# Moving part of a short causal convolution from VectorE to TensorE in a fused delta-rule attention and mixture-of-experts layer

## The chip, the cores and the metric

One core of one Trainium2 chip runs the whole layer in one launch. The metric is the device time of the kernel in microseconds (us). What tells a change of this kernel from no change is about 0.5%.

## The reference, cut to what matters

The layer has two halves. The first is a gated linear attention by the delta rule, the second a router with 32 experts and a shared expert. The change touches only the start of the first half: the projections of the normalised input `x` (2 x 1024 tokens, 512 wide) are convolved along the tokens with four taps that all channels share, and go through SiLU.

```
def _causal_shared_conv(x, w):
    xp = jnp.pad(x, ((0, 0), (K - 1, 0), (0, 0)))
    out = w[0] * xp[:, 0:T, :]
    for j in range(1, K):                      # K = 4 taps
        out = out + w[j] * xp[:, j:j + T, :]
    return out
q = _silu(_causal_shared_conv(x @ Wq, conv_q))
k = _silu(_causal_shared_conv(x @ Wk, conv_k))
v = _silu(_causal_shared_conv(x @ Wv, conv_v))
beta = jax.nn.sigmoid(x @ Wb)
# keys and queries to unit length; per chunk a triangular matrix M of key products is inverted;
# a state S runs over the chunks: u -= w S, o = q S + attn u, S += k^T u; norm, Wo, residual
```

After it come a norm, the router (top groups, top 4 of 32 experts, each expert with room for 80 tokens), the experts and the shared expert.

## The kernel before, in words

**Steps and bodies.** The 1024 tokens are taken in 8 steps of 128 (both batch rows at once). All work is in fp32. A *body* `s` is one turn of the loops on every engine. Body `s` runs the serial core of step `s-1` (four chunks `j` of 32 tokens), prepares step `s` (convolution, SiLU, key products, inverse), projects step `s+1`, and finishes steps `s-2` and `s-3` (output projection, shared expert). Body 0 has no core. Bodies 0 to 7 prepare a step and so hold an inverse; body 8 does not. Then a second block does the routing tables and the 32 experts.

**PE's order is written out by hand.** `FILL` (L64) has 16 strings, four for each chunk of the core. In chunk `j` PE does in this order: state times keys (L497), string `4j`; the solve with the inverse (L512, waits for VectorE's `residual`), string `4j+1`; the state update (L520), string `4j+2`; the output (L526), string `4j+3`. Each letter is a piece of other work: B the beta projection, X the transposes of `x`, P a part of a projection (12 pieces a step, L468; two fill a bank of PSUM), G one quarter of the key and query products (L481), W the output projection (L549), E, F, V, Y the shared expert, H and R for the router, O a small sum. `FILLS` has other strings for single bodies. `Ring` hands six PSUM banks to the pieces in the order in which they stand; a piece waits until the last user of its bank has released it.

**The path of one projection.** PE fills a bank (P). ACT in `take_projection` copies it to `pre` (L703, behind three columns of the step before, the halo) and once more, scaled by the last tap, to `cv` (L704). VectorE adds three taps on `cv` (`conv`, three instructions at L942) and copies the halo (L953). ACT makes the sigmoid in `silu_factor` (Exp, Ln, Exp; L668 to L670). VectorE multiplies: `silu_kq` (L960) for keys and queries, `silu_v` (L965) and then `turn_v` (L968) for values. PE makes the G pieces when both keys and queries are there. VectorE masks them (L980), transposes them for the inverse in `problems` (L985), inverts them with about 30 small instructions and a few large ones (L1017 to L1030), and turns the inverse back (L1044).

**VectorE's order** in a body, as the code has it: `residual(0)` (L1068), conv of keys, conv of queries, `next_state(0)`, `silu_kq` of keys, first tap of values, `silu_kq` of queries, moments of the finished output and `mean_shift` (L1096), `residual(1)`, the other taps of values, masks with `next_state(1)` between them, `problems`, `silu_v`, `turn_v`, `residual(2)`, and the inverse. In body 0 it also does `first_norm(2)` (L916, L929: the layer norm of step 2's input) and scales `wo` (L1205).

**ACT's order** in a body begins with `take_beta`, `take_x`, `take_new(0)`, the sigmoid of keys, the sigmoid of queries, `take_output(0)`, `rstd(1)` (L663), `scale_y`, the first projections, and later the sigmoid of values. Every engine takes its own instructions in this order.

Of the kernel before, what the change touches and what calls it, by code (L numbers as in the profile page):

```python
# [26 lines left out]
P = 128  # L27
# [32 lines left out]

PIECES = dict(X=1, H=1, O=1, G=4, P=12, W=8, E=8, F=8, V=4, Y=4)
BANKS = dict(X=2, H=2, O=2, G=4, P=6, W=2, E=2, F=2, V=1, Y=1)

FILL = ["BXRWW", "WWW", "WWW", "PP", "GPP", "GFF", "GFF", "GFF", "FFPP", "HPP", "PP", "VVVV", "YYYY", "PP", "", "EEEEOEEEE"]  # L64
FILLS = {0: ["BGGGGXPPPPPPPPPPPP"],
         STEPS: ["RWWW", "WWW", "WW", "F", "FF", "F", "F", "FF", "FH", "VV", "V", "VY", "YYY", "EE", "E", "EEOEEE"], STEPS + 1: ["RWWWWWWWWFFFFFFFFHVVVVrYYYYEEEEEEEE"]}


def step_of(body, section):

    if section in "XP":
        return body + 1
    if section in "BG":
        return body
    if section == "O":
        return body - 1
    if section in "WHEr":
        return body - 2
    return body - 3


def pieces_of(body):

    done = dict.fromkeys("BRrXHOGPWEFVY", 0)
# [55 lines left out]
def step_part(nc, ctx, dram, shared):  # L140
# [10 lines left out]
    route_m, pick_of, w_part = shared["route_m"], shared["pick_of"], shared["w_part"]  # L151
    ffn_w, late = shared["ffn_w"], shared["late"]

    wqkv = wring[:, :].rearrange("p (s k n) -> p s k n", s=3, k=KT)
# [104 lines left out]
    v_turned = sem("v_turned")  # L259
    halo_done = sem("halo_done")  # L260
    kq_ready = sem("kq_ready")
# [37 lines left out]
    def quad(n):  # L299
        return slice(DK * n, DK * n + DK)  # L300

    block = ctx.enter_context(nc.Block())
# [130 lines left out]
    def _(pe):  # L433
# [24 lines left out]
        def project(s, n, c):  # L458
# [11 lines left out]
            if c == 1:  # L470
                m.then_inc(ring.full("P", s, n), 1)

        def gram(s, j):

            kq = kqs[s % 2]
            pe.wait_ge(kq_ready, 2 * (s + 1))
            ring.wait_free(pe, "G", s, j)
            bank = ring.bank("G", s, j)
            for i in range(I8):
                for hh in range(HT):  # L480
                    m = te.matmul(bank[quad(hh), i * 64:(i + 1) * 64], kq[quad(hh), i * J + j, 0, :], kq[quad(hh), i * J + j, :, :].rearrange("p a c -> p (a c)"),  # L481
                                  start=True, stop=True)
            m.then_inc(ring.full("G", s, j), 1)
# [118 lines left out]
        def fill_for(body):  # L602
# [3 lines left out]
            def fill(at):  # L606
                for c, step, n in slots[at]:
# [12 lines left out]
                    elif c == "P":  # L620
                        project(step, n // 2, n % 2)
                    elif c == "W":
                        out_proj(step, n // CT, n % CT)
# [20 lines left out]
    def _(act):  # L644
# [46 lines left out]
        def take_projection(s, n):  # L691
# [3 lines left out]
            if s > 0 and half == 0:  # L695
                act.wait_ge(halo_done, 3 * (s - 1) + a + 1)
                if w == 2:
# [4 lines left out]
            bank = ring.bank("P", s, n)[:, :].rearrange("p (i t) -> p i t", t=TT)  # L702
            sc_e.activation(pre[:, w, 4 * half:4 * half + 4, HALO:], bank, ACT.Copy)  # L703
            link(sc_e.activation(cv[:, w, 4 * half:4 * half + 4, :], bank, ACT.Copy, scale=taps[:, w, TAPS - 1:TAPS]))  # L704
            release("P", s, n)
            if half == 1:
                act.sem_inc(pre_ready[w], 1)  # L707

        def silu_factor(s, w):
            act.wait_ge(conv_done[w], s + 1)  # L710
            slot = (1, 0, 2)[w]
            sigmoid(sig[:, slot, :], cv[:, w, :, :].rearrange("p i t -> p (i t)")).then_inc(sig_ready[w], 1)

# [88 lines left out]
        act.wait_ge(taps_in, 16 * 3)  # L802
        for n in range(4):
            take_projection(0, n)
        silu_factor(0, 1)
        take_projection(0, 4)
        silu_factor(0, 0)
        take_projection(0, 5)
        rstd(0, 1)
        take_beta(0)  # L810
        silu_factor(0, 2)
        take_x(1)
        key_norms(0)
        rstd(0, 2)
        for n in range(BANKS["P"]):
# [3 lines left out]
        def body(s):  # L819
# [3 lines left out]
            if new:  # L823
                take_beta(s)
            if nxt:
                take_x(s + 1)
# [15 lines left out]
            if last >= 0:  # L842
                rstd(2, last)
            if new:
                silu_factor(s, 2)
# [49 lines left out]
    def _(dve):  # L895
# [52 lines left out]
        def conv_end(w, s):  # L948
            tap(w, 1)
            tap(w, 2)  # L950
            dve.sem_inc(conv_done[w], 1)

            link(v.tensor_copy(pre[:, w, :, 0:HALO], pre[:, w, :, TT:TT + HALO]))  # L953
            dve.sem_inc(halo_done, 1)

        def silu_kq(a, w, s):

            slot = (1, 0, 2)[w]
            dve.wait_ge(sig_ready[w], s + 1)
            link(v.tensor_tensor(kqs[s % 2][:, :, a, :], flat(cv[:, w, :, :]).rearrange("p (g c) -> p g c", c=CH), sig[:, slot, :].rearrange("p (g c) -> p g c", c=CH), ALU.mult))  # L960
            dve.sem_inc(kq_ready, 1)  # L961

        def silu_v(s):
            dve.wait_ge(sig_ready[2], s + 1)
            link(v.tensor_tensor(flat(cv[:, 2, :, :]), flat(cv[:, 2, :, :]), sig[:, 2, :], ALU.mult))  # L965

# [219 lines left out]
        problems()  # L1186
        row_weights(0)
        inverse_diagonal(range(1, 8))
        silu_v(0)
        turn_v(0)  # L1190
# [10 lines left out]
        dve.wait_ge(small_in, 16 * SMALL)  # L1201
        dve.wait_ge(weights_in, 16 * 4)

        for ct in range(CT):
            last = v.tensor_scalar(wo[:, ct, :], wo[:, ct, :], onw[:, 0:1], None, ALU.mult)  # L1205
        last.then_inc(wo_scaled, 1)
        end_steps()

        def body(s):
# [17 lines left out]
            residual(core, 1)  # L1227
            if new:
                conv_end(2, s)
# [11 lines left out]
            if new:  # L1241
                masks(s, 2)
                masks(s, 3)
                problems()
                silu_v(s)
                turn_v(s)
            residual(core, 2)
# [617 lines left out]
```

## Time and profile before

| what | value |
|---|---|
| median of three runs | 962.0 us (958.39 to 962.54) |
| profiled execution, its own time | 962.78 us |
| span of the profiled execution | 961.0 us |
| PE matmul busy | 822.5 us (86%), 13456 instructions |
| VectorE (DVE) busy | 661.5 us (69%), 1220 instructions |
| ScalarE (ACT) busy | 364.8 us (38%), 683 instructions |
| GpSimd (POOL) busy | 116.7 us (12%), 173 instructions |
| mean granted TensorE clock, as a share of full speed | 0.934 |
| body 1, body 2, body 7 on VectorE | 85.96 to 155.75, 155.75 to 228.74, 536.62 to 611.84 us |

Each engine's busy share is an average over the span. The expert stage begins at about 700 us; there VectorE is nearly idle and PE busy. Before it, in the bodies, both are busy, and which of them a body waits for is read from the timelines.

### The profile page before, as it was taken

The numbers are of one execution on the slowest core, as the hardware profiler recorded it, in microseconds if no ns is written. First come the engines' busy times: TensorE is split into PE (matmuls) and PEld (weight loads), VectorE is DVE, ScalarE is ACT, GpSimd is POOL, SyncE is SP. The second block draws the span as 40 slices with busy tenths as digits, with TensorE's granted clock in tenths as the row PEclk, the third lists the DMA queues.
The fourth block names the chain that finished last, engine by engine and source line by source line (L and its number), as shares of the span: only waits on it lengthen the run. The fifth ranks groups of instructions, "written<-read, shape, count | busy, mean of one in ns | idle before, by whom it ended". The sixth has DMA issues, their size and how long they took to land. (4 is left out here: it accounts for less than half of the span.)

```text
span 961.0 us, 30663 instructions
## 1 busy us (share of the span) xinstructions
PE 822.5 (86%) x13456; PEld 629.2 (65%) x13456; DVE 661.5 (69%) x1220; ACT 364.8 (38%) x683; POOL 116.7 (12%) x173
## 2 busy tenths in 40 slices
PE   6794779789999999999999787998779999999910
PEld 5683665676777777687687464666566887788800
DVE  2799699799789789879877988787691222222238
ACT  2605334435534644544554451332321222222215
POOL 2000000000000000000000000000002454544345
PEclk9895988999999999999999987998889999999965
DMA  8301004300101021020020020020176999999376
GB/s 307 72 23 47 3 3 168 108 3 25 62 18 39 3 69 27 24 70 23 4 69 24 3 70 23 2 89 2 48 286 220 362 362 346 344 360 358 96 266 278
DMA packets 49632, 113.09 MB, mean 118 GB/s; under 512 B 8688, under 2 KB 8816, under 8 KB 49504
## 3 DMA queue, kind: packets, MB, share of 16 engines
q1 hardware_dynamic: 44384, 100.70, 29.1%
q0 software_dynamic: 5120, 10.49, 4.8%
q8 instruction: 104, 1.70, 0.7%
q14 instruction: 24, 0.20, 0.1%
HBM read 84.34 MB, written 26.84 MB: 116 GB/s over the span
## 5 line engine op out<-in xcount | busy, mean ns | idle before, releaser
L468 PE MATMUL bank<-xnT,wring 128*128 128x256 f32 x768 | 183.6, 396 | 2.1 <-ACTq L681 1.3
L468 PEld LDWEIGHTS bank<-xnT,wring 128*128 128x128 f32 x768 | 149.3, 198 | 24.9 <-ACTq L681 1.5
L587 PE MATMUL bank<-late,ffn_w 128*128 128x256 f32 x480 | 117.3, 394 | 0.0
L1754 DVE TENSOR_TENSOR hid<-ps_g,sg 128x160 f32<-128x160 f32 x32 | 10.4, 324 | 148.5 <-ACT sg L1650 148.5
L942 DVE SCALAR_TENSOR_TENSOR cv<-pre,taps,cv 128x1024 f32<-128x1024 f32 x72 | 92.4, 1283 | 18.1 <-ACTq L707 14.4
L587 PEld LDWEIGHTS bank<-late,ffn_w 128*128 128x128 f32 x480 | 90.8, 195 | 15.2 <-issue 1.1
L1509 POOL MEMSET xgT<- 128x512 f32 x2 | 1.0, 532 | 686.9 <-POOLq L1834 686.9
L1609 PEld LDWEIGHTS ps_g<-xgT,wring 128*128 128x128 f32 x640 | 74.4, 192 | 10.9 <-issue 10.9
L1609 PE MATMUL ps_g<-xgT,wring 128*128 128x128 f32 x640 | 74.8, 275 | 1.3 <-ACT xgT L1640 1.3
L1640 ACT ACTIVATE xgT<-ps_x 128x320 f32<-128x320 f32 x32 | 14.0, 437 | 132.8 <-PE ps_x L1598 132.8
L549 PE MATMUL bank<-wo,o_ch 128*128 128x512 f32 x128 | 60.1, 605 | 0.6 <-DVE o_ch L1086 0.6
L481 PE MATMUL bank<-kq 32*32 32x64 f32 x2048 | 42.8, 233 | 16.7 <-DVEq L961 9.1
L598 PE MATMUL bank<-ffn_w,late 128*128 128x512 f32 x112 | 54.5, 628 | 0.1
L703 ACT ACTIVATE pre<-bank 128x512 f32<-128x512 f32 x48 | 28.6, 597 | 67.2 <-PE bank L468 63.7
L481 PEld LDWEIGHTS bank<-kq 32*32 32x32 f32 x2048 | 36.6, 117 | 20.3 <-DVEq L961 11.0
L512 PEld LDWEIGHTS bank<-resid,invT 32*32 32x32 f32 x2048 | 22.0, 110 | 39.9 <-issue 39.8
L512 PE MATMUL bank<-resid,invT 32*32 32x32 f32 x2048 | 25.5, 199 | 24.2 <-DVE resid L1069 24.1
L497 PEld LDWEIGHTS bank<-kq,state 32*32 32x32 f32 x2048 | 32.3, 110 | 20.8 <-issue 11.9
L497 PE MATMUL bank<-kq,state 32*32 32x64 f32 x2048 | 37.7, 224 | 8.4 <-DVE state L1075 7.8
L726 ACT ACTIVATE unew<-bank 128x256 f32<-128x256 f32 x32 | 12.3, 384 | 68.7 <-PE bank L512 68.1
L1618 PE MATMUL ps_y<-wring,hid 128*80 128x512 f32 x80 | 37.7, 593 | 0.2 <-DVE hid L1756 0.2
L980 DVE TENSOR_TENSOR grams<-bank,upto 128x512 f32<-128x512 f32 x32 | 21.8, 682 | 23.0 <-PE bank L481 22.1
(202 smaller groups left out, 1474.2 us busy)
## 6 DMA issues: line engine op xcount, KB each, us to landing
wring<-in_ffn_W_gate SPq DMA_DIRECT2D x20, 512.0 KB, 7.6
wring<-in_ffn_W_up SPq DMA_DIRECT2D x20, 512.0 KB, 9.6
wring<-in_ffn_W_down SPq DMA_DIRECT2D x20, 512.0 KB, 10.7
x_in<-in_attn_x SPq DMA_DIRECT2D x8, 512.0 KB, 3.7
x_res<-in_attn_x SPq DMA_DIRECT2D x8, 512.0 KB, 4.8
side_rows<-late SPq DMA_DIRECT2D x8, 512.0 KB, 7.0
x_rows<-x SPq DMA_DIRECT2D x8, 512.0 KB, 3.2
h_rows<-h SPq DMA_DIRECT2D x8, 512.0 KB, 4.4
```

Of the source, the lines that this page charges most:

```text
L468: m = te.matmul(bank[:, c * COLS:(c + 1) * COLS], wqkv[:, w, kt, ct * P:(ct + 1) * P], xnT[:, kt, :], start=(kt == 0), stop=(kt == KT - 1))
L481: m = te.matmul(bank[quad(hh), i * 64:(i + 1) * 64], kq[quad(hh), i * J + j, 0, :], kq[quad(hh), i * J + j, :, :].rearrange("p a c -> p (a ...
L497: m = te.matmul(here[quad(hh), i * 64:(i + 1) * 64], now[quad(hh), i, :], kq[quad(hh), i * J + j, :, :].rearrange("p a c -> p (a c)"), sta ...
L512: m = te.matmul(aside[quad(hh), i * DK:(i + 1) * DK], invT[quad(hh), i * J + j, :], resid[quad(hh), i, :], start=True, stop=True)
L549: m = te.matmul(bank[:, :], o_ch[:, ct * B + b, :], wo[:, ct, :], start=(ct == 0), stop=(ct == CT - 1))
L587: m = te.matmul(bank[:, c * COLS:(c + 1) * COLS], w[:, kt, ft * P:(ft + 1) * P], hT[:, kt, :], start=(kt == 0), stop=(kt == KT - 1))
L598: m = te.matmul(bank[:, :], sh_h[:, ft, b * TT:(b + 1) * TT], sd_w[:, ft, :], start=(ft == 0), stop=(ft == FT - 1))
L703: sc_e.activation(pre[:, w, 4 * half:4 * half + 4, HALO:], bank, ACT.Copy)
L942: link(v.scalar_tensor_tensor(out=out, in0=pre[:, w, :, n:n + TT], scalar=taps[:, w, n:n + 1], in1=out, op0=ALU.mult, op1=ALU.add))
L980: link(v.tensor_tensor(both, bank, upto[:, :].rearrange("p (a i c) -> p a i c", i=1, a=1).to_broadcast([P, 2, I8, CH]), ALU.mult))
L1609: m = te.matmul(ps_g[q % 2][:, (2 * a + i) * P:(2 * a + i + 1) * P], w[:, k, i * P:(i + 1) * P], xgT[q % 2][:, k, :], start=(k == 0), stop ...
L1618: m = te.matmul(ps_y[q % 2][0:CAP, :], hid[q % 2][:, i, :], w_down[q][:, i, :], start=(i == 0), stop=(i == 1))
```

## The change

Two new kinds of piece, C (keys) and D (values), convolve by matmul. `tap_m` holds, for keys and for values, four 128 x 128 matrices: the identity times one tap. `convolve` multiplies each with `pre`, shifted by 0 to 3 columns, and adds the four products up in a PSUM bank of 512 columns; two banks make one tensor. A piece is two matmul calls, so one tensor is 4 pieces or 8 calls. Values go this way in bodies 0, 1, 2 and 7, keys in body 1: five tensors. For them ACT's second copy of the projection and VectorE's three taps are left out, the sigmoid reads the two banks, and VectorE's product with it is two instructions that read the banks (and then the halo copy). The other bodies are as before.

```
-FILLS = {0: ["BGGGGXPPPPPPPPPPPP"],
+FILLS = {0: ["BGGGGDDDDXPPPPPPPPPPPP"],
+         1: ["BCC", "CCD", "DDD", "X", "GPPPP", "G", "G", "G", "PP", "PP", "PP", "", "", "PP", "", "O"],
+         2: ["BXWW", "WWWD", "WWWD", "DDPP", "GPP", "G", "G", "G", "PP", "HPP", "PP", "", "", "PP", "", "EEEEOEEEE"],
+         STEPS - 1: ["BRWW", "WWW", "WWWD", "DDD", "G", "GFF", "GFF", "GFF", "FF", "H", "", "VVVV", "YYYY", "", "", "EEEEOEEEE"],

# PE
+        def convolve(s, w, n):
+            section, half = "_CD"[w], n // 2
+            if n == 0:
+                pe.wait_ge(tap_mats, 1)
+                pe.wait_ge(pre_ready[w], s + 1)
+            if n % 2 == 0:
+                ring.wait_free(pe, section, s, half)
+            bank = ring.bank(section, s, half)[:, :].rearrange("p (i t) -> p i t", t=TT)
+            for j in range(2 * (n % 2), 2 * (n % 2) + 2):
+                m = te.matmul(bank, tap_m[:, w - 1, j, :], pre[:, w, 4 * half:4 * half + 4, j:j + TT], start=(j == 0), stop=(j == TAPS - 1))
+            if n % 2 == 1:
+                m.then_inc(ring.full(section, s, half), 1)

# ACT, silu_factor
+            if by_matmul(w, s):
+                section, dst = "_CD"[w], sig[:, slot, :]
+                for half in range(2):
+                    ring.wait_full(act, section, s, half)
+                    link(sc_e.activation(dst[:, 512 * half:512 * half + 512], ring.bank(section, s, half)[:, :], ACT.Exp, scale=-1.0))
+                link(sc_e.activation(dst, dst, ACT.Ln, bias=1.0))
+                sc_e.activation(dst, dst, ACT.Exp, scale=-1.0).then_inc(sig_ready[w], 1)
+                return

# ACT, a body (body 1 takes x late and has one more rstd)
-            if nxt:
+            if nxt and s > 1:
                 take_x(s + 1)
...
                 silu_factor(s, 1)
+            if s == 1:
+                rstd(0, 2)
+            if new:
                 silu_factor(s, 0)
             take_output(core, 0)
+            if new and by_matmul(2, s):
+                silu_factor(s, 2)
+            if s == 1:
+                take_x(2)
             if last >= 0:
                 rstd(1, last)

# VectorE, silu_v (silu_kq has the same two halves)
+            if by_matmul(2, s):
+                for half in range(2):
+                    job = "D", s, half
+                    link(v.tensor_tensor(flat(cv[:, 2, 4 * half:4 * half + 4, :]), ring.bank(*job)[:, :], sig[:, 2, 512 * half:512 * half + 512], ALU.mult))
+                    dve.sem_inc(ring.free(*job), 1)
+                halo(2, s)
+                return

# VectorE, body 0
-        conv(0, 1, 0)
+        for half in range(2):
+            conv_half(0, 1, half)
+        halo(1, 0)
         first_moments(1)
-        conv(1, 0, 0)
+        conv_half(1, 0, 0)
         silu_kq(0, 1, 0)
+        conv_half(1, 0, 1)
+        halo(0, 0)
...
-        conv_begin(2, 0)
-        conv_end(2, 0)
         for j in range(J):
             masks(0, j)
+        silu_v(0)
+        turn_v(0)
         problems()
...
-        first_norm(2)
...
-            last = v.tensor_scalar(wo[:, ct, :], wo[:, ct, :], onw[:, 0:1], None, ALU.mult)
-        last.then_inc(wo_scaled, 1)

# VectorE, a body
             if new:
-                conv(0, 1, s)
+                if not by_matmul(1, s):
+                    conv(0, 1, s)
                 conv(1, 0, s)
...
             next_state(core, 0)
+            if s == 1:
+                first_moments(2)
             if new:
                 silu_kq(0, 1, s)
-                conv_begin(2, s)
+                if s == 1:
+                    first_scale(2)
+                if not by_matmul(2, s):
+                    conv_begin(2, s)
                 silu_kq(1, 0, s)
...
             residual(core, 1)
-            if new:
+            if new and by_matmul(2, s):
+                silu_v(s)
+                turn_v(s)
+            elif new:
                 conv_end(2, s)
```

`conv_half` is the three taps on one half of a tensor (512 elements each), so that VectorE can begin in body 0 when the first bank of a projection has been copied. ACT now makes `tap_m` (8 small instructions before its first projection), scales `wo` at the end of body 0, and takes the projections of body 0 in an order that puts the sigmoids earlier. The halo's semaphore is now one for each of the three tensors.

## Rows read from the trace of the kernel before

**Rows 1.** Windows, bodies 1, 2, 7, then part of body 1: length, busy, PEclk, DMA.
```profile
core 0: us, PE busy (x) PEld busy (x) DVE busy (x) ACT busy (x) POOL busy (x), PEclk, DMA share, GB/s
86.00:155.75 69.75, 54.58 (x1404) 43.48 (x1404) 58.87 (x89) 27.19 (x44) 0.00 (x0) 0.82 0.05 16
155.75:228.70 72.95, 62.16 (x1470) 49.74 (x1470) 64.60 (x101) 34.39 (x58) 0.00 (x0) 0.95 0.26 92
536.60:611.80 75.20, 59.61 (x1415) 42.07 (x1414) 63.66 (x97) 28.67 (x49) 0.00 (x0) 0.89 0.09 31
91.00:98.00 7.00, 7.00 (x55) 5.48 (x58) 6.33 (x8) 5.70 (x6) 0.00 (x0) 0.58 0.01 2
```

**Rows 2.** Chain that ended last, first expert's matmuls: start, us, what.
```profile
748.89 3.84 PE ps_g L1609 x32
```

**Rows 3.** Timeline of PE, body 2: start, us, operation, shapes, count, [idle before].
```profile
156.81 0.74 PE L512 MATMUL bank<-resid,invT 32*32 32x32 f32 x64 [1.00 <-DVE resid L1069]
...
164.39 3.72 PE L468 MATMUL bank<-xnT,wring 128*128 128x256 f32 x16
...
169.74 1.10 PE L481 MATMUL bank<-kq 32*32 32x64 f32 x64 [0.60 <-DVEq L961]
...
174.41 0.75 PE L512 MATMUL bank<-resid,invT 32*32 32x32 f32 x64
...
182.48 1.93 PE L481 MATMUL bank<-kq 32*32 32x64 f32 x64
```

**Rows 4.** Timeline of VectorE, body 2, around the last mask.
```profile
184.47 0.69 DVE L980 TENSOR_TENSOR grams<-bank,upto 128x512 f32<-128x512 f32 x1 [2.91 <-PE bank L481]
...
187.26 1.23 DVE L965 TENSOR_TENSOR cv<-cv,sig 128x1024 f32<-128x1024 f32 x1
...
189.91 0.45 DVE L1068 STREAM_TRANSPOSE resid<-bank 128x256 f32<-128x256 f32 x1
```

**Rows 5.** Page, costliest groups: the taps (busy, mean ns, idle before).
```profile
L942 DVE SCALAR_TENSOR_TENSOR cv<-pre,taps,cv 128x1024 f32<-128x1024 f32 x72 | 92.4, 1283 | 18.1 <-ACTq L707 14.4
```

**Rows 6.** Timeline of PE, body 9: eight 512-column calls back to back.
```profile
663.28 7.03 PE L549 MATMUL bank<-wo,o_ch 128*128 128x512 f32 x16
```

**Rows 7.** Timeline of ACT, body 0.
```profile
16.60 0.60 ACT L703 ACTIVATE pre<-bank 128x512 f32<-128x512 f32 x1 [6.09 <-PE bank L468]
...
23.42 0.60 ACT L703 ACTIVATE pre<-bank 128x512 f32<-128x512 f32 x1 [2.28 <-PE bank L468]
...
28.24 1.06 ACT L668 ACTIVATE sig<-cv 128x1024 f32<-128x1024 f32 x1 [0.19 <-ACT cv L704]
```

**Rows 8.** Timeline of PE, body 0: the four G pieces.
```profile
40.03 6.41 PE L481 MATMUL bank<-kq 32*32 32x64 f32 x256 [4.46 <-DVEq L961]
```

**Rows 9.** Timeline of VectorE, body 0.
```profile
47.83 1.93 DVE L985 STREAM_TRANSPOSE inv_pad<-grams 128x1024 f32<-128x1024 f32 x1
...
70.48 1.29 DVE L916 BATCH_NORM_STATS2 stats<-x_in 128x6 f32<-128x512 f32 x2
...
72.65 1.00 DVE L929 TENSOR_SCALAR x_in<-x_in,mv,rs 128x512 f32<-128x512 f32 x2 [0.60 <-ACT rs L664]
...
84.37 1.67 DVE L1205 TENSOR_SCALAR wo<-wo,onw 128x512 f32<-128x512 f32 x4 [0.23 <-DVE invT L1044]
```

**Rows 10.** Timeline of PE, body 1.
```profile
87.00 1.08 PE L512 MATMUL bank<-resid,invT 32*32 32x32 f32 x64 [11.27 <-DVE resid L1069]
...
91.45 6.36 PE L468 MATMUL bank<-xnT,wring 128*128 128x256 f32 x16
...
104.61 0.75 PE L512 MATMUL bank<-resid,invT 32*32 32x32 f32 x64
```

**Rows 11.** Timeline of VectorE, body 1.
```profile
113.10 0.69 DVE L980 TENSOR_TENSOR grams<-bank,upto 128x512 f32<-128x512 f32 x1 [2.88 <-PE bank L481]
...
118.60 0.45 DVE L1068 STREAM_TRANSPOSE resid<-bank 128x256 f32<-128x256 f32 x1
```

**Rows 12.** Timeline of VectorE, body 7.
```profile
552.88 0.16 DVE L1096 SCALAR_TENSOR_TENSOR shift<-mv,rs 128x2 f32<-128x2 f32 x1 [0.60 <-ACT rs L664]
...
564.42 0.69 DVE L980 TENSOR_TENSOR grams<-bank,upto 128x512 f32<-128x512 f32 x1 [2.00 <-PE bank L481]
```

More of the change, by code:

```diff
@@ L82, in pieces_of @@
 def pieces_of(body):
-    done = dict.fromkeys("BRrXHOGPWEFVY", 0)
+    done = dict.fromkeys("BRrXHOGPCDWEFVY", 0)
     slots = []
@@ L259, in step_part @@
     v_turned = sem("v_turned")
-    halo_done = sem("halo_done")
+    halo_done = [sem(f"halo_done{n}") for n in range(3)]
+    pre_half = sem("pre_half")
+    tap_mats = sem("tap_mats")
     kq_ready = sem("kq_ready")
@@ L300, in quad, with by_matmul @@
         return slice(DK * n, DK * n + DK)
+    def by_matmul(w, s):
+        return (w == 1 and s in CONV_K) or (w == 2 and s in CONV_V)
     block = ctx.enter_context(nc.Block())
@@ L621, in fill @@
                         project(step, n // 2, n % 2)
+                    elif c in "CD":
+                        convolve(step, "_CD".index(c), n)
                     elif c == "W":
@@ L702, in take_projection @@
             bank = ring.bank("P", s, n)[:, :].rearrange("p (i t) -> p i t", t=TT)
-            sc_e.activation(pre[:, w, 4 * half:4 * half + 4, HALO:], bank, ACT.Copy)
-            link(sc_e.activation(cv[:, w, 4 * half:4 * half + 4, :], bank, ACT.Copy, scale=taps[:, w, TAPS - 1:TAPS]))
+            if by_matmul(w, s):
+                link(sc_e.activation(pre[:, w, 4 * half:4 * half + 4, HALO:], bank, ACT.Copy))
+            else:
+                sc_e.activation(pre[:, w, 4 * half:4 * half + 4, HALO:], bank, ACT.Copy)
+                link(sc_e.activation(cv[:, w, 4 * half:4 * half + 4, :], bank, ACT.Copy, scale=taps[:, w, TAPS - 1:TAPS]))
             release("P", s, n)
+            if s == 0 and half == 0:
+                act.sem_inc(pre_half, 1)
             if half == 1:
@@ L802, in _ @@
         act.wait_ge(taps_in, 16 * 3)
-        for n in range(4):
+        for n in range(2):
+            for j in range(TAPS):
+                last = sc_e.activation(tap_m[:, n, j, :], ident[:, :], ACT.Copy, scale=taps[:, n + 1, j:j + 1])
+        last.then_inc(tap_mats, 1)
+        for n in range(3):
             take_projection(0, n)
         silu_factor(0, 1)
+        take_projection(0, 3)
+        rstd(0, 1)
+        silu_factor(0, 0)
         take_projection(0, 4)
-        silu_factor(0, 0)
         take_projection(0, 5)
-        rstd(0, 1)
         take_beta(0)
@@ L813, in _ @@
         key_norms(0)
-        rstd(0, 2)
+        act.wait_ge(small_in, 16 * SMALL)
+        act.wait_ge(weights_in, 16 * 4)
+        for ct in range(CT):
+            last = sc_e.activation(wo[:, ct, :], wo[:, ct, :], ACT.Copy, scale=onw[:, 0:1])
+        last.then_inc(wo_scaled, 1)
         for n in range(BANKS["P"]):
@@ L843, in body @@
                 rstd(2, last)
-            if new:
+            if new and not by_matmul(2, s):
                 silu_factor(s, 2)
@@ L951, in conv_end, with halo, conv_half @@
             dve.sem_inc(conv_done[w], 1)
+            halo(w, s)
+        def halo(w, s):
+            if by_matmul(w, s):
+                ring.wait_full(dve, "_CD"[w], s, 1)
             link(v.tensor_copy(pre[:, w, :, 0:HALO], pre[:, w, :, TT:TT + HALO]))
-            dve.sem_inc(halo_done, 1)
+            dve.sem_inc(halo_done[w], 1)
+        def conv_half(a, w, half):
+            i = slice(4 * half, 4 * half + 4)
+            if half == 0:
+                dve.wait_ge(pre_half, a + 1)
+            else:
+                dve.wait_ge(pre_ready[w], 1)
+            for n in range(TAPS - 1):
+                link(v.scalar_tensor_tensor(out=cv[:, w, i, :], in0=pre[:, w, i, n:n + TT], scalar=taps[:, w, n:n + 1], in1=cv[:, w, i, :], op0=ALU.mult, op1=ALU.add))
+            if half == 1:
+                dve.sem_inc(conv_done[w], 1)
         def silu_kq(a, w, s):
@@ L1174, in _ @@
         dve.wait_ge(taps_in, 16 * 3)
-        conv(0, 1, 0)
+        for half in range(2):
+            conv_half(0, 1, half)
+        halo(1, 0)
         first_moments(1)
-        conv(1, 0, 0)
+        conv_half(1, 0, 0)
         silu_kq(0, 1, 0)
+        conv_half(1, 0, 1)
+        halo(0, 0)
         turn_k(0)
@@ L1244, in body @@
                 problems()
-                silu_v(s)
-                turn_v(s)
+                if not by_matmul(2, s):
+                    silu_v(s)
+                    turn_v(s)
             residual(core, 2)
```

28 lines of the change are left out of this document (17 added, 11 removed).

## The prediction

> **What bounds the kernel now.** I read four views in this order. The chain that ended last shows that from the first expert on PE sets the end by itself [rows 2]; nothing there is changed, so whatever the bodies gain or lose shifts that chain and arrives at the end in full. The busy time by windows, a window for each touched body, shows VectorE busy 58.9 of 69.8 us in body 1, 64.6 of 73.0 in body 2, 63.7 of 75.2 in body 7, and PE 54.6, 62.2 and 59.6 [rows 1]. That looks like a VectorE-bound loop, and the timelines are needed to see that it is so in one half of a body only. In body 2 PE runs from its first solve at 156.81 to the end of the last G piece at 184.41 with a single wait for VectorE, 0.60 us [rows 3], and VectorE stands idle 2.91 us before its last mask, waiting for that G piece [rows 4]. So up to the last G piece PE sets the pace; after it the inverse does, on VectorE, and PE waits. Body 1 has the same wait, 2.88 us [rows 11], and body 7 one of 2.00 us [rows 12]. All five convolutions by matmul are put in front of the G pieces, into the half that PE paces, or between them and VectorE's inverse (body 0).
>
> **The price of one tensor.** VectorE loses three taps of 1.283 us, 3.85 us [rows 5]. PE gains 8 calls of 512 columns. The row of eight such calls has 16 records (an fp32 call makes two) in 7.03 us [rows 6]: 0.88 us a call, 1.76 us a piece, 7.03 us a tensor at full clock. The strided right-hand side does not appear before; I bound it from below by this row and from above by twice it, 14.1 us, which is what the lower clock costs (below), and take 7.03.
> The Trainium skill ("TensorE: Matmul & The Clock Gate", Back-to-back issue gap) gives 512 columns as N/2.4 + 2.5 ns, 0.216 us, and by it the eight calls would be an estimated 1.7 us. The row disagrees by a factor of four; "FP8 and Floating Point Precision" (TensorE Precision Notes) says true FP32 takes four passes, which fits the row. The measurement decides.
>
> **Body 2, the cleanest.** Four D pieces enter PE's order before the last G. PE has there only the 0.60 us wait to hide them in, so the last G ends 7.03 - 0.60 = 6.4 us later. VectorE's freed 3.85 us fall into its own wait, and become wait. What it does gain is that `silu_v` and `turn_v` now stand ahead of the masks, inside the wait, instead of after `problems`: from 187.26 to 189.91, 2.65 us [rows 4]. Net for `residual(2)`, and for all behind it: 6.4 - 2.65 = **+3.8 us**. The new wait on ACT (the values' sigmoid before `rstd(1)`, so `mean_shift` and `residual(1)` queue behind it) costs about 3 us on VectorE, but PE reaches its second solve only 6.4 us later anyway, so it is covered.
>
> **Body 7.** Here PE has air, as there are no P pieces: it waits before the first key products and the G pieces. But the second D bank is full only when PE has done its W pieces, one D, the output and DDD: by the piece's 1.76 us that is 1.8 + 5.3 us behind the point near 546 at which the output ends now, 553.1. The sigmoid of values then takes a half Exp of 0.60 and a full Ln and Exp of 1.06 each plus links [rows 7], to about 556.1, and only then ACT does `rstd(1)`. `mean_shift`, at 552.88 before [rows 12], comes at about 556.6, +3.7; `residual(1)` and the solve follow it. From there PE needs 9.5 to 10.4 us to the last G as before. The last mask, at 564.42, comes at 567 to 568, about +2.7, and 2.65 us of `silu_v` and `turn_v` are again gone behind it. Net **+0.2 us** (bounds -1.5 and +2).
>
> **Body 0.** Gains first. The banks of a projection come 3.41 us apart ((23.42 - 16.60)/2, [rows 7]). With halves, the taps of keys end at 23.4, and with sigmoids taken earlier `silu_kq` of queries ends at about 36.0, four before the G pieces' present start of 40.03. They took 6.41 us after a wait of 4.46 [rows 8], 4 x 1.10 at full clock [rows 3]; I take 5, as PE has been idle only half a microsecond. Then DDDD, 7.03: to 48.1. Sigmoid to 50.9 (one half Exp, then 2 x 1.09), `silu_v` in two halves of 0.69 with links, halo, `turn_v`: 3.4 us. `problems` starts at 54.3 instead of 47.83 [rows 9]: +6.5. VectorE has nothing else to do in that wait; its masks are over at about 42. Behind it fall away `silu_v` and `turn_v` (2.65), `first_norm(2)` (from 70.48 to 1.00 after 72.65, 3.1 with its links) and the scaling of `wo` (0.23 + 1.67, less an overlap, 1.65) [rows 9]. ACT takes the last over while it is idle. Net **-0.9 us**; if G and D run at half clock for one stretch, up to +3.5; if G takes 4.4, -1.5. P for step 1 ends near 73 instead of 69.7, in PE's 11.27 us wait [rows 10].
>
> **Body 1.** It starts on VectorE at 85.1. Two C pieces lie in PE's wait, free. CCD comes between the first solve and the state update: PE is at half clock there (0.58 granted in 91 to 98, [rows 1]; 16 records of 256 columns took 6.36 us [rows 10] against 3.72 [rows 3]), so 5.3 becomes 7.6 us. `next_state(0)` waits for it until 95.5, and VectorE, which now has only one convolution before it, idles some 5 us. `first_norm(2)` moved here begins after it, and ACT's `rstd(0,2)` stands in front of the queries' sigmoid, so the queries are ready at 102.6 instead of 99.8. PE meanwhile does DDD to 100.8, output, X, keys: G0 from 103.7. The P pieces of step 2 need `take_x(2)`, which ACT does after the values' sigmoid, at 107.0. PPPP (7.44) follows in place of PP, and the second solve is at 114.4 instead of 104.61. From that solve the last mask came 8.5 us later [rows 10, 11]; so 122.9 instead of 113.10, +9.8, less 2.65: `residual(2)` at 125.7 against 118.60 [rows 11]. That is +7.1 on the clock, **+8.0 us** for the body itself. The 37.1 us behind it are VectorE's and unchanged.
>
> **Sum.** -0.9 + 8.0 + 3.8 + 0.2 = +11.1 us. Against the profiled execution (962.78 of device time, span 961.0) that is 973.9; that run stands 0.8 above the median of the runs shown, so 973.
>
> **Rivals.** *The clock gives something back.* The added matmuls fill PE's holes, and PE stands at half clock in holes now: 0.82 mean in body 1 [rows 1]. If CCD ran at full clock, body 1 would lose 2.6 us less (6.36 - 3.72), and the second half about as much again in bodies 1 and 7, in all some 5: 968. For: fewer holes. Against: 6 us of hole remain ahead of the first solve. The Trainium skill ("TensorE: Matmul & The Clock Gate", the HAM clock gate) says that idle is the throttled state and activity releases it, which agrees with the windows and with both readings.
> *The instruction gaps close.* From the second solve to the last G's end body 2 takes 10.0 us [rows 3], for a solve, an update and an output of 0.75 each and three G pieces of 1.10, 5.6 us. If the missing 4.4 us are a lack of instructions, and the long matmuls ahead let them pile up, bodies 1 and 2 win up to 3 us each: 967. Against: PP stands in front of these pieces now already.
> *Body 0 goes cold.* G at 6.41 and D at half clock: +3.5 instead of -0.9, so 978.
> *PE's added work is hidden, and VectorE's relief counts* (the other side). Place: the stretch before the last G. It decides by the price of one tensor on PE: below 0.60 + 2.65 = 3.25 us (0.41 a call) body 2 turns to a gain. With no price at all: body 0 some -8.6, body 1 -6.9 (2.65, and 4.25 of the keys' convolution and halo), bodies 2 and 7 -2.65 each, -20.8 in all: 942. For: VectorE's busy share in all three bodies. Against: rows 3 and 6.
> *The holes are deeper than I read them*, and the sum cancels: 962.
>
> **Chances.** Forecast (968 to 978) 0.60; clock or gaps give back (963 to 968) 0.15; body 0 cold or another wait, above 978, 0.08; cancels, 0.06; hidden on PE, 942 to 957, 0.11. Time 973, the likeliest; range 962 to 980 (0.60 + 0.15 + about 0.05). A change below 0.5%, 957.2 to 966.8, is what a measurement of this kernel can't tell from none. Faster by more 0.12, within 0.13, slower by more 0.75.
>
> **What would show it.** Right: in the changed profile body 2's last mask stands some 6.4 us later after the start of the body with VectorE's idle time there ended by a G piece, and `residual(2)` 3.8 us later; the convolve group has 80 records of 512 columns at 0.44 us each; body 0 has an idle of 8 to 9 us on VectorE ahead of `silu_v`, ended by ACT; bodies 3 to 6, which are not touched, keep their length. Wrong: VectorE's idle ahead of the last mask no longer than before, or convolve calls well under 0.88 us.

## The result, and the profile after

| | before | changed |
|---|---|---|
| median of 20 runs, us | 962.56 (958.39 to 968.97) | 966.46 (963.86 to 969.48) |
| profiled execution: own time, span | 962.78, 961.0 | 964.57, 962.8 |
| PE busy | 822.5 | 844.0 |
| VectorE busy | 661.5 | 643.0 |

The ratio is 1.0039, 95% interval [1.0025, 1.0054]: 3.8 us slower where 11 were forecast. The page of the changed kernel, sections 1 and 5 (engine or operation, busy us, share and count; in section 5 mean ns of one and the idle time before):

```profile
PE 844.0 (88%) x13535; PEld 633.2 (66%) x13536; DVE 643.0 (67%) x1212; ACT 364.7 (38%) x690; POOL 116.8 (12%) x173
...
L1001 DVE SCALAR_TENSOR_TENSOR cv<-pre,taps,cv 128x1024 f32<-128x1024 f32 x51 | 65.5, 1283 | 2.5
...
L497 PE MATMUL bank<-pre,pick_of 128*128 128x512 f32 x80 | 38.1, 621 | 0.0
```

The group of full taps went from 72 [rows 5] to 51: 15 taps, those of the five tensors, have left VectorE, and the other 6 are now the twelve half taps of keys and queries in body 0. 80 records have come to PE (the 621 ns are each record's own length; they overlap). The windows of the touched bodies, to be read against [rows 1]; the last is the stretch of CCD in body 1, for which half clock had been forecast:

```profile
core 0: us, PE busy (x) PEld busy (x) DVE busy (x) ACT busy (x) POOL busy (x), PEclk, DMA share, GB/s
86.84:165.77 78.93, 62.03 (x1436) 45.06 (x1436) 53.99 (x90) 27.91 (x48) 0.00 (x0) 0.91 0.05 16
165.77:241.75 75.98, 68.04 (x1485) 51.90 (x1486) 61.15 (x99) 34.58 (x59) 0.00 (x0) 0.96 0.25 88
543.59:615.51 71.92, 62.84 (x1430) 41.32 (x1428) 59.98 (x95) 29.06 (x50) 0.00 (x0) 0.98 0.10 32
88.60:95.60 7.00, 7.00 (x20) 2.81 (x17) 3.09 (x4) 2.41 (x4) 0.00 (x0) 0.76 0.01 2
```

A body is measured from the first operation of `residual(0)` on VectorE to that of the next body, so the whole difference can be laid out (us):

| stretch | before | changed | difference | forecast |
|---|---|---|---|---|
| start of body 1 | 85.96 | 86.84 | +0.9 | -0.9 |
| body 1 | 69.8 | 78.9 | +9.1 | +8.0 |
| body 2 | 73.0 | 76.0 | +3.0 | +3.8 |
| bodies 3 to 6, not touched | 307.9 | 301.8 | **-6.0** | 0 |
| body 7 | 75.2 | 71.9 | **-3.3** | +0.2 |
| body 8 to the end | 349.2 | 347.3 | -1.9 | 0 |

Up to body 2 each stretch is within 1.8 us of its forecast. More than half of what came back, 6.0 of 11.2 us, came in bodies for which both kernels hold the same instructions (only numbers of semaphores and banks differ), and in which the granted clock is 1.00 in both. Here is PE in body 3 of the kernel before, then of the changed one, each from the second solve on (start, us, operation, count, [idle before, ended by]):

```profile
247.39 0.75 PE L512 MATMUL bank<-resid,invT 32*32 32x32 f32 x64
...
249.81 0.53 PE L481 MATMUL bank<-kq 32*32 32x64 f32 x22 [0.99 <-issue]
...
253.74 0.65 PE L481 MATMUL bank<-kq 32*32 32x64 f32 x31 [0.28 <-issue]
...
257.59 0.76 PE L481 MATMUL bank<-kq 32*32 32x64 f32 x39 [0.19 <-issue]
...
266.60 0.75 PE L512 MATMUL bank<-resid,invT 32*32 32x32 f32 x64
```

```profile
260.41 0.75 PE L540 MATMUL bank<-resid,invT 32*32 32x32 f32 x64
261.02 1.09 PE L509 MATMUL bank<-kq 32*32 32x64 f32 x64
...
264.73 1.09 PE L509 MATMUL bank<-kq 32*32 32x64 f32 x64
...
268.28 1.10 PE L509 MATMUL bank<-kq 32*32 32x64 f32 x64
...
277.63 0.75 PE L540 MATMUL bank<-resid,invT 32*32 32x32 f32 x64
```

Before, each G piece is broken by a hole that "issue" ends, which means that the profile shows nothing that PE waited for; the changed kernel runs its pieces whole, and the same work takes 17.22 us instead of 19.21. Count the matmuls between two holes of the first fence: 22, then 8 (F) and 64 (update) that the dots leave out, then the first 33 of the next G piece, 127; from the second hole to the third 128. With a weight load for each, that is a block of 256 instructions.

### The profile page after: what moved, and what is told of

The parts are those of the page before. It is cut to its first block and busy times, and to the rows that moved or that the text cites. A ratio compares the mean times of both kernels' runs of the same rounds, so it can differ in the third digit from the quotient of the medians.

```text
span 962.8 us, 30837 instructions
## 1 busy us (share of the span) xinstructions
PE 844.0 (88%) x13535; PEld 633.2 (66%) x13536; DVE 643.0 (67%) x1212; ACT 364.7 (38%) x690; POOL 116.8 (12%) x173
## 5 line engine op out<-in xcount | busy, mean ns | idle before, releaser
L615 PE MATMUL bank<-late,ffn_w 128*128 128x256 f32 x480 | 115.1, 388 | 0.5 <-issue 0.5
L1706 PEld LDWEIGHTS ps_g<-xgT,wring 128*128 128x128 f32 x640 | 74.4, 192 | 10.9 <-issue 10.9
L1706 PE MATMUL ps_g<-xgT,wring 128*128 128x128 f32 x640 | 74.8, 275 | 1.3 <-ACT xgT L1737 1.3
L1001 DVE SCALAR_TENSOR_TENSOR cv<-pre,taps,cv 128x1024 f32<-128x1024 f32 x51 | 65.5, 1283 | 2.5
L736 ACT ACTIVATE pre<-bank 128x512 f32<-128x512 f32 x38 | 22.7, 596 | 55.0 <-PE bank L482 53.7
L509 PE MATMUL bank<-kq 32*32 32x64 f32 x2048 | 35.4, 216 | 6.0 <-issue 4.5
L497 PE MATMUL bank<-pre,pick_of 128*128 128x512 f32 x80 | 38.1, 621 | 0.0
L577 PEld LDWEIGHTS bank<-wo,o_ch 128*128 128x128 f32 x128 | 22.5, 190 | 21.9 <-issue 20.1
L509 PEld LDWEIGHTS bank<-kq 32*32 32x32 f32 x2048 | 31.0, 105 | 7.6 <-issue 4.9
```

Of the source, the lines that this page charges most:

```text
L497: m = te.matmul(bank, tap_m[:, w - 1, j, :], pre[:, w, 4 * half:4 * half + 4, j:j + TT], start=(j == 0), stop=(j == TAPS - 1))
L577: m = te.matmul(bank[:, :], o_ch[:, ct * B + b, :], wo[:, ct, :], start=(ct == 0), stop=(ct == CT - 1))
L615: m = te.matmul(bank[:, c * COLS:(c + 1) * COLS], w[:, kt, ft * P:(ft + 1) * P], hT[:, kt, :], start=(kt == 0), stop=(kt == KT - 1))
L1001: link(v.scalar_tensor_tensor(out=out, in0=pre[:, w, :, n:n + TT], scalar=taps[:, w, n:n + 1], in1=out, op0=ALU.mult, op1=ALU.add))
L1706: m = te.matmul(ps_g[q % 2][:, (2 * a + i) * P:(2 * a + i + 1) * P], w[:, k, i * P:(i + 1) * P], xgT[q % 2][:, k, :], start=(k == 0), stop ...
```

## The experiments

Theory A, formed on this trace: PE's instructions arrive in blocks of 256, and where a border falls into a dense run of 32-row matmuls PE runs dry. By body 3 the change has put 32 calls (64 matmul records and 64 loads, 128 instructions) ahead, and so has moved every border behind it by half a block. Rival B: something else that the changed kernel has beside its convolutions, the ring of banks or the halo's semaphores, made these bodies shorter. Rival R: the convolutions themselves speed up what follows (the clock, or VectorE's relief in body 7). Rival N: noise between executions. The lengths of single bodies are read from one profiled execution of each kernel. With the borders of the changed kernel, bodies 3 to 6 took 301.5 to 304.1 us in five such executions (changed, e3, e6, e7, e9), so differences below some 2 us are not read from them.

**Moving the borders and nothing else.** Small matmuls stand in front of all work, in PE's wait for the first input (7.9 us). A call makes 4 instructions.

```
         pe.wait_ge(first_consts, 1)
+        for _ in range(32):      # e1 on the kernel before, e2 on the changed one
+            te.matmul(ring.banks[5][0:32, 0:32], ident[0:32, 0:32], ident[0:32, 0:32], start=True, stop=True)
         turn_x(0)
```

> The kernel before with 32 small matmul calls (128 PE instructions, 32 x 32, identity times identity into a bank that is overwritten later) ahead of the first transposes, where PE waits for the input; nothing else differs. Theory A: PE gets its instructions in blocks of 256, and the holes in its dense stretches stand at block borders, so what counts is where the borders fall. 128 instructions is what the changed kernel has more by body 3, so bodies 3 to 6 should take 75.2 to 75.9 us each as in the changed kernel (307.9 before, 301.8 after), the holes inside the G pieces of bodies 3 to 6 go, and the time falls by about 6 us, ratio 0.994. Rival B: bodies 3 to 6 became shorter through the ring of PSUM banks or the halo semaphores of the changed kernel; then this kernel keeps 307 to 308 us there and ratio 1.000.

> The changed kernel with the same 128 instructions in front, which puts the block borders of bodies 3 to 6 back to about where the kernel before has them (256 more in all). Theory A: the holes come back, bodies 3 to 6 take about 308 us instead of 301.8, and the time is about 6 us above the changed kernel's, ratio to the kernel before 1.010. Rival B: no change against the changed kernel, 301 to 302 us there, ratio 1.004.

Measured: e1, which only does more work, is *faster* than the kernel before, 0.9916 [0.9883, 0.995]; e2 is slower than the changed one, 1.0103 [1.0074, 1.0133]. Bodies 3 to 6 changed places: 301.8 us in e1, 307.2 in e2, and body 7 likewise, 72.4 and 74.8. PE of e1 in body 3 has the whole pieces of the changed kernel:

```profile
247.08 1.10 PE L481 MATMUL bank<-kq 32*32 32x64 f32 x64
...
250.63 1.10 PE L481 MATMUL bank<-kq 32*32 32x64 f32 x64
...
254.25 1.10 PE L481 MATMUL bank<-kq 32*32 32x64 f32 x64
```

All three rivals fall: nothing of the change is in e1, everything of it is in e2, and both ratios have moved beyond their intervals.

**The period.** 64 instructions (e4) and 256 (e5) in front of the kernel before.

```
-        for _ in range(32):
+        for _ in range(16):      # e4; range(64) in e5
```

> The kernel before with 16 such calls, 64 instructions, a border a quarter of a block earlier. Theory A: each body moves by where its borders fall; the holes in bodies 3 to 6 move 32 records earlier, out of the G pieces' middle into the solve and the state update or the P pieces; total between the kernel before and the one with 128, ratio 0.993 to 1.000. Rival B: 1.000.

> The kernel before with 64 small calls, 256 PE instructions, in front. Theory A says that the borders repeat every 256 instructions, so this one must look like the kernel before and not like the one with 128: bodies 3 to 6 about 307 to 308 us, ratio 1.000 (0.997 to 1.003). A rival by which any added work at the start helps (a warmer clock, a later start of the projections) expects at least what 128 instructions gave, ratio 0.992 or less.

e4: 0.993 [0.9905, 0.9956], bodies 3 to 6 303.6. e5: 1.0018 [0.9994, 1.0042], 307.5, and body 3 of e5 is broken again in the same G pieces, after 43, 34 and 25 matmuls, where the kernel before breaks after 42, 33 and 25:

```profile
254.11 0.53 PE L481 MATMUL bank<-kq 32*32 32x64 f32 x21 [1.00 <-issue]
...
258.04 0.64 PE L481 MATMUL bank<-kq 32*32 32x64 f32 x30 [0.23 <-issue]
...
261.88 0.76 PE L481 MATMUL bank<-kq 32*32 32x64 f32 x39 [0.19 <-issue]
```

Half a block takes the holes away, a whole block brings them back: the period is 256 instructions. A rival by which any added work at the start helps falls with it, since e5 adds twice as much as e1 and gains nothing.

**Parts of the change.** Body 7 without its D pieces:

```
-CONV_V = (0, 1, 2, STEPS - 1)
+CONV_V = (0, 1, 2)
-         STEPS - 1: ["BRWW", "WWW", "WWWD", "DDD", "G", ...],
```

> The changed kernel with body 7's values convolved on VectorE and its old strings; the stream before body 7 is the same. If the change itself shortens body 7 (71.9 us in the changed kernel, 75.2 before), this kernel has 75.2 there and is 3.3 us slower than the changed one, ratio to the kernel before 1.007. If body 7 got its time from the block borders or the clock alone, body 7 stays near 72 to 73 and the ratio at 1.004 to 1.005. The forecast's reading (+0.2 for body 7 by its own) expects no difference between this and the changed kernel.

Ratio 1.0064 [1.0042, 1.0086]; body 7 takes 72.0 us, with them 71.9, and e1, which has nothing of the change, 72.4. The D pieces of body 7 are worth nothing there, as forecast (+0.2); its 3.3 us are the border's. That the ratio lies above the changed kernel's 1.0039 is not from body 7: bodies 3 to 6, with the same instructions and borders, took 1.6 us more in this execution, and body 8 to the end 1.8 more. Where the border costs body 7 of the kernel before shows in its second half:

```profile
594.26 0.52 PE L526 MATMUL bank<-grams,unew 32*32 32x32 f32 x37 [1.24 <-issue]
594.72 5.41 PE L587 MATMUL bank<-late,ffn_w 128*128 128x256 f32 x16
```

A hole of 1.24 us stands there, and behind it the granted clock is 0.71 (594.2 to 600) and 16 records take 5.41 us; e1 has no hole at this place, a clock of 1.00, and 3.72 for the same records. All five kernels in which body 7 has a hole of more than 1 us there (before, e5, e12, e13, e14) take 75.1 to 76.5 us for the body, the other twelve 71.9 to 74.8.

Body 1 without C and D, but still with the norm and the X piece of step 2 late; fillers in front keep the later borders where they were:

```
-CONV_K = (1,)
-CONV_V = (0, 1, 2, STEPS - 1)
+CONV_K = ()
+CONV_V = (0, 2, STEPS - 1)
-         1: ["BCC", "CCD", "DDD", "X", "GPPPP", ...],
+         1: ["B", "", "", "X", "GPPPP", ...],
```

> The changed kernel without body 1's C and D pieces (16 calls less there, 16 small ones in front instead, so that the stream from body 2 on has the same borders); keys and values of body 1 are convolved on VectorE again, step 2's norm and its late transposes stay in body 1. If the two convolutions on PE are what costs in body 1, as forecast, body 1 falls from 78.9 us to 70 or 71 and the time by 8 us, ratio 0.996. If it is the late transposes and the PPPP behind them, body 1 stays at 76 or more and the time falls by 3 us at most.

A miss for me: I expected 70 to 71 us for the body, and it took 77.6 (ratio 1.0023 [1.0001, 1.0045]). The convolutions can be taken out and the body stays long; 2.65 us of that are `silu_v` and `turn_v`, which stand behind the masks again. PE of e6 shows what holds it:

```profile
99.77 1.97 PE L459 MATMUL bank<-ident,x_in 128*128 128x128 f32 x8 [8.37 <-DVE x_in L990]
...
104.42 7.17 PE L482 MATMUL bank<-xnT,wring 128*128 128x256 f32 x32
111.52 0.75 PE L540 MATMUL bank<-resid,invT 32*32 32x32 f32 x64
```

X waits 8.37 us for the moved norm, all four P pieces stand behind it, and the second solve behind them. So the opposite, the convolutions kept and X early:

```
-         1: ["BCC", "CCD", "DDD", "X", "GPPPP", ...],
+         1: ["BXCC", "CCD", "DDD", "PP", "GPP", ...],
+            (and the norm of step 2 back in body 0)
```

> The changed kernel with step 2's norm back in body 0 and its transposes first in body 1, so that PP, GPP follow the DDD as in the kernel before; all five convolutions stay on PE. The run without body 1's convolutions left body 1 at 77.6 of 78.9 us, so the late transposes were enough for that length. If the two costs lie one over the other (either alone makes body 1 long), body 1 is 75 to 77 us here too and body 1 starts 3.1 us later; ratio 1.003 to 1.006. If the late transposes are the only cost and the convolutions fit into PE's waits, body 1 is 69 to 71 us and the time falls by 4 to 5 us even with the later start, ratio 0.999.

Body 1: 74.6 us, just under the 75 to 77 expected. The length of body 1 also depends on where the borders fall in it: the kernel before takes 69.8, 71.5, 68.2 and 72.6 us with 0, 64, 128 and 192 instructions in front, and e7 (below), which has the convolutions and the late X, only 75.2 where the changed kernel takes 78.9. So the four lengths (69.8 with neither, 77.6 with the late X alone, 74.6 with the convolutions alone, 78.9 with both) don't price the two causes. The start of the second solve on PE, ahead of most holes, is steadier. Behind the start of the body it stands at 18.7 to 20.3 us with neither, 25.6 with the late X alone, 24.7 with the convolutions alone, and 29.0 to 29.7 with both: against the kernel before, +6.9 and +6.0 apart and +11.0 together, so each is enough to delay it and they overlap in part only. The kernel as a whole gains nothing by e9, 1.0046 [1.0027, 1.0064], since body 1 starts at 89.0 instead of 86.8, body 7 takes 73.6 and body 8 to the end 1.3 more.

Body 2 without D:

```
-CONV_V = (0, 1, 2, STEPS - 1)
+CONV_V = (0, 1, STEPS - 1)
-         2: ["BXWW", "WWWD", "WWWD", "DDPP", ...],
```

> The changed kernel without body 2's D pieces (8 calls less there, 8 small ones in front instead); values of body 2 on VectorE. By the forecast body 2 gives back 3.8 us: 76.0 falls to 72 to 73, ratio 1.000. If PE's four extra pieces were hidden there, nothing changes: 1.004.

Body 2: 73.2 us against 76.0 (74.8 to 75.6 in e3, e6 and e9); ratio 0.9995 [0.9972, 1.0018]. The D pieces cost it 1.6 to 2.8 us. The ratio fell by more than that because body 1, where the same pieces meet the borders 32 instructions off, took 75.2 instead of 78.9 (the holes between its second solve and its last mask add up to 1.1 us instead of 3.7), and the bodies from 3 on took some of it back.

**The new start of body 0 alone**: halves of keys and queries, earlier sigmoids, the scaling of `wo` on ACT, but no convolution by matmul and no moved norm.

```
+CONV_K = CONV_V = ()
+FILLS[0] = ["BGGGGXPPPPPPPPPPPP"]   (and no entries for bodies 1, 2 and 7)
+32 calls in front
```

> No convolution by matmul at all: the kernel before with only the new start of body 0 (the convolution of keys and queries in halves, sigmoids earlier, the scaling of the output weights on ACT) and 32 small calls in front. The new start brings the queries 3.5 to 4 us earlier and takes 1.65 us of scaling off VectorE, so body 1 should start at 80.5 to 81.5 instead of 85.6, and the time should be 4 to 5 us under the kernel before with 32 calls: ratio 0.986 to 0.988. If the sum for body 0 was wrong and its start does not matter (a DMA or the projections set it), 0.992.

0.9874 [0.9834, 0.9914]. `problems` and the start of body 1 on VectorE, to be read against [rows 9], 47.83, and a start at 85.96:

```profile
45.11 1.92 DVE L1073 STREAM_TRANSPOSE inv_pad<-grams 128x1024 f32<-128x1024 f32 x1
...
81.65 0.45 DVE L1156 STREAM_TRANSPOSE resid<-bank 128x256 f32<-128x256 f32 x1 [0.23 <-DVE invT L1132]
```

4 us are gained, and kept. The rest is the border's, and a scan over it looks for the best place: 24, 40 and 48 calls.

```
-        for _ in range(32):
+        for _ in range(24):      # e10; 40 in e11, 48 in e12
```

> Only the new start of body 0, with 24 small calls (96 instructions) in front instead of 32. The borders lie 32 instructions later than with 128 in front. If they decide, bodies 1 to 7 differ by 1 to 8 us from those of the kernel with 32 (sum of bodies 3 to 6 302 to 308); ratio to the kernel before 0.985 to 0.995.

> The same start with 40 small calls (160 instructions). 0.983 to 0.993 by the place of the borders; equal to the kernel with 32 (0.987) if 32 instructions do not move a border into or out of a dense stretch.

> The same start with 48 small calls (192 instructions). 0.983 to 0.995 by the place of the borders.

0.9868 [0.9835, 0.9901], **0.985 [0.9818, 0.9883]** and 0.9986 [0.9966, 1.0005]. e11 (947.5 us, bodies 3 to 6 301.6) beats both kernels, but can't be told from e8 and e10, whose intervals overlap with its own; e12, eight calls further, has the holes back (307.0).

**What the change costs at equal borders.** Three more runs close the table: 48 calls on the kernel before, 16 and 48 on the changed one.

```
-        for _ in range(32):
+        for _ in range(48):      # e13 before, e15 changed; 16 in e14, changed
```

> The kernel before with 48 small calls (192 instructions) in front. By the borders it lies between the places of 128 and of 256: 0.992 to 1.002. Bodies 3 to 6 about 307, as the new start with 48 calls had (306.99).

> The changed kernel with 64 instructions in front. Its bodies 3 to 6 have the borders of the kernel before with 192: about 307 us. If the forecast's size holds on the mean of four places, the mean of the changed kernel's ratios lies 0.010 to 0.013 above that of the kernel before; if the two places so far were chance, 0.004 to 0.008. This run alone 1.008 to 1.013.

> The changed kernel with 192 instructions in front; its bodies 3 to 6 have the borders of the kernel before with 64 (303.6 us). This run alone 1.003 to 1.010; the mean as said for the run with 64.

| instructions in front | 0 | 64 | 128 | 192 | mean |
|---|---|---|---|---|---|
| before | 1 | 0.993 [0.9905, 0.9956] | 0.9916 [0.9883, 0.995] | 1.0006 [0.9986, 1.0027] | 0.9963 |
| changed | 1.0039 [1.0025, 1.0054] | 1.0108 [1.0078, 1.0137] | 1.0103 [1.0074, 1.0133] | 1.0056 [1.0035, 1.0077] | 1.0077 |
| bodies 3 to 6, before | 307.9 | 303.6 | 301.8 | 307.4 | |
| bodies 3 to 6, changed | 301.8 | 306.6 | 307.2 | 303.0 | |

The rows of bodies 3 to 6 are the same curve, shifted by half a block. Each column alone mixes the change with its border; the means do so much less. Their difference is 0.0114, or 10.9 us, uncertain by about 0.0017 (the seven half-intervals in quadrature, over four). The same eight ratios, taken as pairs whose borders agree behind body 2 (the changed kernel at n, the one before at n + 128, counted modulo 256), give +0.0123, +0.0102, +0.0103 and +0.0126 for n of 0, 64, 128 and 192: no pair stands out. By stretches, the means of the four profiled executions of each kernel are (us):

| stretch | before | changed | difference | forecast |
|---|---|---|---|---|
| start of body 1 | 86.0 | 86.5 | +0.5 | -0.9 |
| body 1 | 70.5 | 78.6 | +8.1 | +8.0 |
| body 2 | 73.9 | 76.4 | +2.4 | +3.8 |
| bodies 3 to 6 | 305.2 | 304.7 | -0.5 | 0 |
| body 7 | 73.8 | 74.1 | +0.3 | +0.2 |
| body 8 to the end | 348.7 | 348.2 | -0.5 | 0 |

## Why the prediction was wrong

The failed step is the one that says that bodies 3 to 6, "which are not touched, keep their length", and so the zero that stood in the sum for all that is outside the touched bodies. They gave 6.0 us, body 7 gave 3.3 by the same cause, and the stretch from body 8 on 1.9. The terms for the change itself hold in their sum: +11.1 were forecast, and the means over four placements differ by 10.9 ± 1.6. (By stretches, the start of body 1 came 1.4 us above its forecast and body 2 1.4 below; these two cancel.) The change costs 11 us, and the place where it happened to put PE's block borders gave 7 of them back. That the time of 966.5 us still lies in the range, in the part (963 to 968) that was kept for "the clock or the gaps give something back", is luck: there the clock, or gaps closing in bodies 1 and 2, were to do it, and the time came back in bodies 3 to 7 and behind them.

The evidence lay in the trace of before. The rival "the instruction gaps close" saw 4.4 us missing between the second solve and the last G of body 2 and asked whether long matmuls ahead would fill them. In body 2 the gaps between the second solve and the last G add up to 3.9 us before and 3.5 changed, so there they did not close. The right question was what sets their *place*: a count of matmuls between two "issue" rows gives 128, and then any change in the number of PE's instructions moves all holes behind it.

Point by point:

- **The price of a tensor** is right. In body 0, the first of these rows, 16 records take 7.13 us, 0.89 us a call (forecast 0.88). At the low clock in body 1 the next row, 12 records, takes 7.08 us; the window above shows a clock of 0.76 there, and 7.6 had been forecast (5.3 and the 2.6 that the rival adds for half clock would be 7.9). At full clock 12 records take 5.42 (the last row).

```profile
42.56 7.13 PE L497 MATMUL bank<-pre,pick_of 128*128 128x512 f32 x16
...
88.56 7.08 PE L497 MATMUL bank<-pre,pick_of 128*128 128x512 f32 x12
...
96.25 5.42 PE L497 MATMUL bank<-pre,pick_of 128*128 128x512 f32 x12
```

- **Body 0.** VectorE idles 9.22 us ahead of `silu_v`, ended by ACT (forecast 8 to 9), and `problems` starts at 56.00, 1.7 later than forecast:

```profile
52.60 1.53 DVE L1053 TENSOR_TENSOR cv<-bank,sig 128x512 f32<-128x512 f32 x2 [9.22 <-ACT sig L752]
...
56.00 1.94 DVE L1077 STREAM_TRANSPOSE inv_pad<-grams 128x1024 f32<-128x1024 f32 x1
```

  In this execution ACT's first copy came at 17.54 instead of 16.60 [rows 7], 0.9 late, by a wait for PE's first bank; over the seventeen traces it comes between 15.6 and 17.8, so single starts carry that much scatter. Over the profiled executions, body 1 starts at 85.2 to 87.0 in the seven kernels that have the changed body 0, 86.1 in the mean, and at 85.6 to 87.2, 86.2 in the mean, in the five that have the old one (forecast -0.9, measured -0.1; +0.5 over the four placements of each kernel alone). Its parts, taken from differences between single executions: the new start gains 4.0 us (e8), the norm's leaving 3.1 [rows 9], and the convolution by matmul costs 7.4, the 89.01 of e9, which has it and the norm in body 0, against the 81.65 of e8.
- **Body 1** is right in size (+9.1, in the mean of four placements +8.1; forecast +8.0) and half right in its reason. The second solve was forecast 29.3 us behind the start of the body and came 29.7 behind it (116.53), the last mask 8.5 after that and came 8.8 after. VectorE waits for it first for the state update and then for the G piece:

```profile
120.65 0.42 DVE L1167 TENSOR_TENSOR state<-state,bank 128x256 f32<-128x256 f32 x1 [10.22 <-PE bank L548]
...
125.31 0.69 DVE L1072 TENSOR_TENSOR grams<-bank,upto 128x512 f32<-128x512 f32 x1 [2.80 <-PE bank L509]
```

  I had told it as one chain that starts at CCD. e6 shows that the chain over the moved norm, `take_x(2)`, X and PPPP makes 6.9 of the 11.0 us by which the second solve comes later even without the convolutions, and e9 that the convolutions make 6.0 without the late X.
- **Body 2** is right: +3.0, in the mean of four placements +2.4 (forecast +3.8). The last mask stands 34.3 us behind the start of the body instead of 28.7, +5.6 (forecast +6.4), its idle ended by the G piece; the wait for `rstd(1)` is there too, and is covered as forecast:

```profile
185.44 0.16 DVE L1188 SCALAR_TENSOR_TENSOR shift<-mv,rs 128x2 f32<-128x2 f32 x1 [4.14 <-ACT rs L694]
...
200.06 0.69 DVE L1072 TENSOR_TENSOR grams<-bank,upto 128x512 f32<-128x512 f32 x1 [3.37 <-PE bank L509]
```

- **Body 7** is right in its own effect (e3). `mean_shift`, forecast 3.7 us late, stands 19.6 us behind the start of the body, 16.3 before, +3.3, and `silu_v` in the wait gives it back:

```profile
563.19 0.16 DVE L1188 SCALAR_TENSOR_TENSOR shift<-mv,rs 128x2 f32<-128x2 f32 x1 [4.06 <-ACT rs L694]
...
573.75 0.69 DVE L1072 TENSOR_TENSOR grams<-bank,upto 128x512 f32<-128x512 f32 x1 [0.71 <-PE bank L509]
```

**Of the rivals**, "hidden on PE" is refuted (e7, and the means over four placements), "body 0 goes cold" by the 7.13. "The clock gives something back" has a grain of truth: the granted clock of bodies 1 and 7 rose from 0.82 and 0.89 to 0.91 and 0.98. But CCD saved only 0.5 us of its 7.6, and body 7 is about as short in e1, at 0.91 and without the change. "The holes are deeper than I read them", by which the sum would cancel, is refuted by the means over four placements, 11 us apart.

What stays open: how far ahead PE's instructions are fetched, and so why most borders under long matmuls show no hole, was not measured by itself; nor were the 1.9 us from body 8 on (0.5 in the mean of four placements, where single executions of the changed kernel differ by up to 4.9) and the 0.9 us of the first bank followed to a cause.

## What to carry to other kernels

Before you forecast zero for what a change does not touch, look for "issue" rows in the timeline of the engine that sets the pace, and count the instructions between two of them: if it is a fixed number, every added or removed instruction moves all later holes, and effects of 1% have to be compared over several placements (here 0, 64, 128, 192 instructions in front). Where such holes cost, a few idle instructions put into a wait at the start are a cheap thing to tune. And moving work from an engine that is busy in the mean to one that paces the half in which it lands costs its full price there (the second solve of body 2 came 6.6 us later for 7.0 us of matmuls), however idle it looks over the loop.

## What the runs showed of the hardware

PE takes its instructions in blocks of 256. The changed kernel's page shows 27,071 instructions on PE and PEld and 104 packets of 1.70 MB in the instruction queue, one for 260 instructions, 16.4 kB each. Over the seventeen kernels the packets step with the count: 104 in every one of up to 27,104 instructions (e13), 105 in every one from 27,136 = 106 x 256 on (e14). Holes stand 128 matmuls apart, and 256 instructions in front bring them back to their places. Two neighbouring holes in dense 32-row stretches of the two kernels stand 3.6 to 4.1 us apart (108.49 and 112.06 in body 1 before; 120.06, 123.75 and 127.72 after), though PE is busy for only 1.7 us of the first such stretch after (120.06 to 121.74). Here PE of the changed kernel in body 1:

```profile
120.06 0.54 PE L548 MATMUL bank<-unew,k_tok 32*32 32x32 f32 x40 [1.64 <-issue]
...
123.75 0.55 PE L554 MATMUL bank<-grams,unew 32*32 32x32 f32 x40 [2.01 <-issue]
...
127.72 0.77 PE L525 MATMUL bank<-kq,state 32*32 32x64 f32 x41 [2.14 <-issue]
```

The Trainium skill ("Runtime: NRT & Kernel Launch", Instruction fetch mechanics) states the same block of 256 instructions but calls the cost of a crossing "mostly hidden". The runs agree on the block and not on the cost: the same kernel, with nothing but its borders moved, runs at 0.9916 to 1.0018 of its time, and with the new start at 0.985 to 0.9986.
